# First W1 part of all eight experts loaded early and the chosen one copied; lower halves placed two blocks further

## The reference

```
# end of layer 0:  x = x + experts64(layernorm(x))        (router: layernorm(x) @ router_w.T)
# layer 1:
xn  = layernorm(x)
x   = x + gnn(xn) + mix(xn)        # gnn: agg @ W_conv, Wq, Wk, Wv, Wo, proj;  mix: w_qkv, w_proj
# last part of layer 1, E = 8, K = 2, FF = 2048
xe     = layernorm(x)
logits = xe @ Wg + bg
w, idx = top_k(logits, 2);  w = softmax(w)
h = silu(xe @ W1[e] + b1[e])       # W1: [8, 512, 2048]
y = h @ W2[e] + b2[e]              # W2: [8, 2048, 512]
out = x + sum over the two chosen e of w * y
```

## Time and profile before

| | us |
|---|---|
| median of 3 runs | 845.24 |
| lowest and highest of them | 845.07, 846.45 |
| the profiled execution | 843.48 |
| its span, first to last instruction | 841.7 |
| around the span | 1.78 |

### The profile page before, as it was taken

How to read it: one execution, slowest core, us unless ns; L and a number is a source line. 1 busy time by engine, 2 the same in 40 slices (tenths; PEclk the granted TensorE clock), 3 DMA queues, 4 the chain that set the end, 5 groups by cost and what they waited for, 6 DMA issues and landing times.

```text
span 841.7 us, 10823 instructions
## 1 busy us (share of the span) xinstructions
PE 800.7 (95%) x3995; PEld 640.9 (76%) x3995; DVE 539.5 (64%) x743; ACT 248.6 (30%) x468; POOL 148.2 (18%) x96
## 2 busy tenths in 40 slices
PE   4999999999999999999998999997699999999997
PEld 3988766847477777765767778897598888888886
DVE  5876998979989999999777426068541111511112
ACT  4252223316411013222045332142432321432310
POOL 2011001120100000002201350031343330433300
PEclk9999999999999998999999999999589999999999
DMA  7533779796878768742041120000242120322001
GB/s 245 213 50 47 227 214 337 266 276 158 240 228 276 246 220 282 242 139 100 1 159 58 48 97 1 1 2 1 100 151 96 55 98 2 100 100 100 0 0 61
DMA packets 64211, 110.21 MB, mean 131 GB/s; under 512 B 6815, under 2 KB 16412, under 8 KB 64172
## 3 DMA queue, kind: packets, MB, share of 16 engines
q1 hardware_dynamic: 54476, 96.71, 34.5%
q0 software_dynamic: 6912, 7.70, 5.4%
q10 hardware_dynamic: 2784, 5.27, 1.7%
HBM read 105.81 MB, written 1.28 MB: 127 GB/s over the span
## 4 chain that ended last, share of the span: by engine, by line
PE 89%; DVE 6%; issue 2%; ACT 1%; POOL 1%; DVEq 0%; POOLq 0%
PE bank L1310 55%; PE bank L1730 13%; PE bank L1396 6%; PE bank L1511 4%; PE bank L1528 3%; PE bank L1522 2%; PE bank L1505 2%; PE bank L1326 1%; DVE st L890 1%; PE bank L1437 1%; PE bank L1333 1%; DVE slot L987 1%; ACT slot L581 1%; DVE slot L885 0%; DVE slot L1116 0%
## 5 line engine op out<-in xcount | busy, mean ns | idle before, releaser
L1004 DVE SCALAR_TENSOR_TENSOR weights<-weights,att 128x2048 f32<-128x2048 f32 x116 | 268.9, 2392 | 2.7 <-DMA weights<-in_L_gnn_basis 2.1
L1291 DVE CAST hid_hi<-slot 128x626 fp32r<-128x626 f32 x32 | 15.6, 487 | 160.7 <-ACT slot L846 160.7
L1310 PE MATMUL bank<-half,ew_hi 128*128 128x314 f32 (+1 forms) x512 | 114.0, 312 | 2.2 <-POOL ew_lo L550 2.2
L1310 PE MATMUL bank<-AT,slot 125*128 125x312 f32 (+1 forms) x400 | 105.9, 426 | 0.8 <-ACT slot L711 0.8
L1310 PEld LDWEIGHTS bank<-AT,slot 125*128 125x128 f32 x400 | 75.5, 189 | 31.0 <-ACT slot L711 1.0
L550 POOL TENSOR_TENSOR ew_lo<-weights,ew_hi 128x1024 fp32r<-128x1024 f32 x28 | 69.4, 2500 | 134.4 <-ACT ew_hi L828 134.4
L1310 PEld LDWEIGHTS bank<-half,ew_hi 128*128 128x128 f32 x512 | 88.4, 193 | 5.6 <-issue 2.9
L581 ACT ACTIVATE slot<-bank 128x312 f32<-128x312 f32 (+6 forms) x88 | 43.8, 525 | 148.7 <-PE bank L1310 128.9
L1310 PE MATMUL bank<-weights,slot 128*125 128x512 f32 (+5 forms) x306 | 86.9, 447 | 0.3 <-ACT slot L581 0.3
L846 ACT ACTIVATE slot<-bank,eb_now 128x312 f32<-128x312 f32 x64 | 33.3, 522 | 157.2 <-PE bank L1310 157.2
L1310 PE MATMUL bank<-half,ew_lo 128*128 128x312 f32 (+1 forms) x256 | 79.5, 310 | 0.0
(11 more groups left out here) (297 smaller groups left out, 1116.4 us busy)
## 6 DMA issues: line engine op xcount, KB each, us to landing
weights<-in_L_gnn_basis SPq DMA_DIRECT2D x60, 1024.0 KB, 5.5
weights<-in_L_ffn_W SPq DMA_DIRECT2D x32, 512.0 KB, 4.5
weights<-in_L_mix_kqv_w SPq DMA_DIRECT2D x1, 3072.0 KB, 10.2
weights<-in_w_qkvT SPq DMA_DIRECT2D x3, 1024.0 KB, 5.4
slot<-slot POOLq DMA_DIRECT2D x10, 250.0 KB, 6.5
weights<-in_L_mix_mlp_w ACTq DMA_DIRECT2D x2, 1024.0 KB, 13.6
weights<-in_L_gnn_root ACTq DMA_DIRECT2D x2, 1024.0 KB, 8.7
slot<-in_row_mlp_b POOLq DMA_DIRECT2D x1, 1250.0 KB, 26.1
```

Of the source, the lines that this page charges most:

```text
L1004: ins = dve.scalar_tensor_tensor(wrel[layer][r], wmat(at), att[:, layer, r, b:b + 1], wrel[layer][r], ALU.mult, ALU.add)
L1310: ins = pe.matmul(out, a, b, start=i == 0, stop=i == len(pairs) - 1)
```

## The change

1. SP, once the product `xq` is complete, loads W1[e, :, 0:256] of all eight experts (512 KB each) to `candidates`, columns 8192 to 16383 of `weights`. When the list is there, it leaves out the W1 load of chunk 0 of the first expert.
2. DVE, behind the write of the expert numbers and ahead of the count, waits for these loads and for `lin_split` 4, reads the first expert's number into a register and copies its 1024 columns to raw chunk 0; the copy signals `ew_in0` in the place of the transfer.
3. So that `candidates` covers nothing live, the low part of block i lies at block (i + 2) % 4 of `ew_lo`, for the matrices and for the experts' chunks; `conv_hi` and `conv_lo` move to blocks 0 and 1.
4. Since `conv_hi` now lies where `o2` still reads, POOL's split of W_conv waits for `psum_full` at `filled("o2", 5)`, that is for the last tile of `o2`, where it waited for `o2_low` 4.

```
-        conv_hi, conv_lo = (ew_lo[:, b, :]... for b in (1, 2))
+        conv_hi, conv_lo = (ew_lo[:, b, :]... for b in (0, 1))
+        def low_block(i):
+            return ew_lo[:, (i + 2) % 4, :]
+        candidates = weights[:, 8192:8192 + 1024 * E1]
...
+            sp.wait_ge(S("psum_full"), filled("xq", 8))
+            for e in range(E1):
+                load(candidates[:, 1024 * e:1024 * e + 1024].rearrange("p (k f) -> p k f", k=KT),
+                     I["L1_ffn_W1"][e, :, 0:256].rearrange("(k p) f -> p k f", p=128), "cand_in")
             sp.wait_ge(S("elist"), 1)
             sp.wait_ge(S("lin_split"), 4)
...
-            def load_chunk(e, c):
+            def load_chunk(e, c, first=False):
                 w1c, w2c = raw1(c), raw2(c)
-                sp.dma_start(w1c, ...).then_inc(S(f"ew_in{c % 2}"), 16)
+                if not first:
+                    sp.dma_start(w1c, ...).then_inc(S(f"ew_in{c % 2}"), 16)
                 sp.dma_start(w2c, ...).then_inc(S(f"ew2_in{c % 2}"), 16)
...
             pool.wait_ge(S("Wconv_in"), 16)
-            pool.wait_ge(S("o2_low"), 4)
+            pool.wait_ge(S("psum_full"), filled("o2", 5))
             link(pool.tensor_copy(conv_hi, W_conv))
             pool.tensor_tensor(conv_lo, W_conv, conv_hi.bitcast(f32), ALU.subtract).then_inc(S("conv_split"), 1)
...
             dve.tensor_copy(el_i[0:1, 0:8], key1).then_inc(S("elist"), 1)
             dve.wait_ge(S("elist"), 1)
+            dve.wait_ge(S("cand_in"), 16 * E1)
+            dve.wait_ge(S("lin_split"), 4)
+            e = dve.value_load(el_i[0:1, 0:1], min_val=0, max_val=E1 - 1)
+            dve.tensor_copy(weights[:, 0:1024], candidates[:, bass.ds(1024 * e, 1024)]).then_inc(S("ew_in0"), 16)
             link(dve.tensor_scalar(srt, srt, 0.5, None, ALU.is_ge))
...
-                dve.tensor_tensor(ew_lo[:, 1, :], weights[:, 2048:4096], ew_hi[:, 1, :].bitcast(f32), ALU.subtract)...
+                dve.tensor_tensor(low_block(1), weights[:, 2048:4096], ew_hi[:, 1, :].bitcast(f32), ALU.subtract)...
```

More of the change, by code:

```diff
@@ L226, in gps_two_layers @@
         xb_hi, xb_lo = half[5], half[3]
-        conv_hi, conv_lo = (ew_lo[:, b, :].rearrange("p (k n) -> p k n", k=KT) for b in (1, 2))
+        conv_hi, conv_lo = (ew_lo[:, b, :].rearrange("p (k n) -> p k n", k=KT) for b in (0, 1))
         Z_AT = (5, 6)
@@ L232, in gps_two_layers, with lin_hi, lin_lo @@
         h1 = col(4)
-        def lin(t, name):
-            return t[:, LIN[name], :].rearrange("p (k n) -> p k n", k=KT)
+        def low_block(i):
+            return ew_lo[:, (i + 2) % 4, :]
+        candidates = weights[:, 8192:8192 + 1024 * E1]
+        def lin_hi(name):
+            return ew_hi[:, LIN[name], :].rearrange("p (k n) -> p k n", k=KT)
+        def lin_lo(name):
+            return low_block(LIN[name]).rearrange("p (k n) -> p k n", k=KT)
         def wait_split(eng, it, c, part=1):
@@ L249, in raw2, with w1_half, w2_half @@
             return wmat(2048 * (c % 2) + 1024, 2, H)
[L251 to L256, removed]
+        def w1_half(block, f):
+            return block[:, 0:1024].rearrange("p (k f) -> p k f", k=KT)[:, :, 128 * (f % 2):128 * (f % 2) + 128]
+        def w2_half(block, f):
+            return block[:, 1024 + H * (f % 2):1024 + H * (f % 2) + H]
         eb1 = sb("eb1", [128, E1 * F1 // 128])
@@ L412, in _ @@
             w2v = I["L1_ffn_W2"].rearrange("e (f p) n -> e p f n", p=128)
-            def load_chunk(e, c):
+            def load_chunk(e, c, first=False):
                 w1c, w2c = raw1(c), raw2(c)
-                sp.dma_start(w1c, w1v[bass.ds(e, 1), :, :, 256 * c:256 * c + 256].rearrange("o p k f -> (o p) k f")).then_inc(S(f"ew_in{c % 2}"), 16)
+                if not first:
+                    sp.dma_start(w1c, w1v[bass.ds(e, 1), :, :, 256 * c:256 * c + 256].rearrange("o p k f -> (o p) k f")).then_inc(S(f"ew_in{c % 2}"), 16)
                 sp.dma_start(w2c, w2v[bass.ds(e, 1), :, 2 * c:2 * c + 2, :].rearrange("o p f n -> (o p) f n")).then_inc(S(f"ew2_in{c % 2}"), 16)
@@ L423, in _ @@
                     wait_split(sp, 0, c - 2)
-                load_chunk(e, c)
+                load_chunk(e, c, first=c == 0)
             sp.wait_ge(S("elist"), 2)
@@ L511, in split_linear @@
             def split_linear(i, used):
-                hi, lo = (t[:, LIN[LIN_ORDER[i]], :] for t in (ew_hi, ew_lo))
+                hi, lo = ew_hi[:, LIN[LIN_ORDER[i]], :], low_block(LIN[LIN_ORDER[i]])
                 raw = weights[:, 2048 * (i % 2):2048 * (i % 2) + 2048]
@@ L549, in _ @@
                         pool.wait_ge(S("ew_high"), 16 * it + (2 * c + part + 1))
-                        pool.tensor_tensor(ew_lo[:, c % 4, at:at + 1024], weights[:, 2048 * (c % 2) + at:2048 * (c % 2) + at + 1024],
+                        pool.tensor_tensor(low_block(c)[:, at:at + 1024], weights[:, 2048 * (c % 2) + at:2048 * (c % 2) + at + 1024],
                                            ew_hi[:, c % 4, at:at + 1024].bitcast(f32), ALU.subtract).then_inc(S("ew_split"), 1)
@@ L1286, in _ @@
                 dve.wait_ge(S("ew_high"), 16 * it + 4)
-                dve.tensor_tensor(ew_lo[:, 1, :], weights[:, 2048:4096], ew_hi[:, 1, :].bitcast(f32), ALU.subtract).then_inc(S("ew_split1"), 1)
+                dve.tensor_tensor(low_block(1), weights[:, 2048:4096], ew_hi[:, 1, :].bitcast(f32), ALU.subtract).then_inc(S("ew_split1"), 1)
                 for f in range(16):
@@ L1360, in split_rows_out @@
             def split_rows_out(stage, name):
-                wh, wl = lin(ew_hi, name), lin(ew_lo, name)
+                wh, wl = lin_hi(name), lin_lo(name)
                 for j in range(TT):
@@ L1660, in _ @@
                 m, (a, w) = by_half(n)
-                split_cols(claim(pe, "xq", n), lin(ew_hi, "q"), lin(ew_lo, "q"), hid_hi, hid_lo, m, a).then_inc(S("psum_full"), 1)
+                split_cols(claim(pe, "xq", n), lin_hi("q"), lin_lo("q"), hid_hi, hid_lo, m, a).then_inc(S("psum_full"), 1)
             pe.wait_ge(S("xkv_out"), 1)
@@ L1673, in projected @@
                 pe.wait_ge(S("xo_low"), 4 * (n // 4) + 4)
-                split_cols(bk, lin(ew_hi, "proj"), lin(ew_lo, "proj"), hid_hi, hid_lo, m, a).then_inc(S("psum_full"), 1)
+                split_cols(bk, lin_hi("proj"), lin_lo("proj"), hid_hi, hid_lo, m, a).then_inc(S("psum_full"), 1)
             def sum_row(j):
@@ L1727, in output @@
                         hh, hl = (t[:, f % 4, P * j:P * j + P] for t in (hid_hi, hid_lo))
-                        products = ((hh, w2_half(ew_hi, f)), (hh, w2_half(ew_lo, f)), (hl, w2_half(ew_hi, f)))
+                        wh, wl = w2_half(ew_hi[:, f // 2 % 4, :], f), w2_half(low_block(f // 2), f)
+                        products = ((hh, wh), (hh, wl), (hl, wh))
                         for i, (a, b) in enumerate(products):
@@ L1740, in _ @@
                         pe.wait_ge(S("eh_out"), 32 * it + max(n - 2, 0) + 1)
-                        wh, wl = w1_half(ew_hi, f), w1_half(ew_lo, f)
+                        wh, wl = w1_half(ew_hi[:, f // 2 % 4, :], f), w1_half(low_block(f // 2), f)
                         group(B("eh", n % 3)[:, 0:w], [(wt[:, k, :], xt[:, k, a:a + w]) for k in range(KT)
```

## The result

Four runs of the changed kernel gave 852.37 us in the median (851.88 to 852.95), four of the kernel before 845.40 (845.07 to 846.45): a ratio of 1.0096, with a 95% interval of 1.0071 to 1.0122. The change makes the kernel slower. Measured once more beside later experiments, the ratio was 1.0048 (1.0030 to 1.0066). Where the runs of a kernel fall into groups the two can differ: e1's medians lie 3.4 us apart and its ratio is 1.0069, e6's lie 6.2 us apart and its ratio is 0.9958. The profiled execution took 852.95 us, its span 851.2.

The account below looks back on a forecast made before the run. The chain of work that ended last was taken as PE for 89% and DVE for 6%. Copy 1.5 + hold of DVE 3.1 + clock 1.0 = 5.6 us, against 845.24 giving 850.8 us; range 846.5 to 853.5.

Parts of the forecast that it names:

- a fall that covers a third of it: Router's stretch, 426.23 to 429.88 us: PE falls to 1.2 GHz for a third of it, 1.0 us.
- the rival with the fall over the whole stretch: Router's stretch: half clock throughout (2.9 us), or POOL keeps DVE out through both instructions (4.9 us); 852.7 us, chance 0.15.
- The hold of DVE: End of layer 0: POOL's late W_conv split blocks DVE's normalisations, delaying tile 3's transposes 3.1 us; ends 0 and 4.9.
- the second step: End of layer 0: tile 3's normalisation waits for POOL's subtraction until 428.85 us, ending near 429.2 instead of 426.09.
- The clock: Router's stretch: 3.6 us of idle PE may bring half clock; taken as 1.0 us, at most 2.9, at least 0.
- The copy: Start of the experts: DVE's register load (0.8) and copy (0.69) go wholly on the path, 1.5 us; ends 1.0 and 2.2.
- The loads at nothing: Behind the xq product: eight 512 KB loads on idle wires, some 38 us ahead of the expert list, cost nothing.
- the blocks at nothing: Low blocks in ew_lo: same engines, sizes and order, so the new places cost nothing.
- The early W1 off the path: Start of the experts: W1 had landed 1.7 us before ACT began, so loading it early gains the first product nothing.
- The ceiling I gave it, 1.06 us: Ahead of ACT's first high part: the most to be had if W1's landing did hold ACT, 1.06 us.
- The experts' start against the clock's rise, taken as 0: Experts' loop: it starts at another moment against the clock's rise; about 1 us either way, taken as 0.
- The rival in which L885 gets by: Router's stretch: DVE's normalisation is not held by POOL, only the copy's 1.5 us is left; 846.7 us, chance 0.11.

Follow-up runs that it names:

- e1: Kernel before with one line changed: POOL's W_conv split waits for the last o2 tile; no loads, copy or new blocks; 848.63 us, ratio 1.0069.
- e6: Layout of e2 without DVE's copy: ACT and POOL split the first expert's W1 chunk 0 straight from the candidates, ahead of the loop; 838.87 us, ratio 0.9958.
- e7: Changed kernel with 13 extra products on PE in the router's pause, ahead of the transposes of tile 3; 847.64 us, ratio 1.0045.
- e10: Kernel before with e1's late split and e7's 13 extra PE products in the pause, no loads or copy; 844.81 us, ratio 1.0004.
- e5: Changed kernel with POOL's late cast and subtraction of W_conv each cut into four pieces of 512 columns; 847.18 us, ratio 1.0033.
- e2: Changed kernel with the W_conv split back at its old time and blocks, the matrices' low parts in other blocks; 844.52 us, ratio 1.0009.
- e3: As e2, with DVE's register load and copy moved behind the write of the combination weights; 844.59 us against the kernel before, ratio 1.0001.
- e8: As e6, with extra PE products in the pauses from the expert transposes to the b2 products; 835.66 us, ratio 0.9910 against the kernel before.

## Why the prediction came out as it did

The direction was right, the mechanisms were those named, and the time, 852.37 us, lies inside the range of 846.5 to 853.5. The forecast of 850.8 was 1.6 us short, and the step at fault is one term of the sum: "I take 1.0, a fall that covers a third of it". It measured 3.4 us. No row stood behind the third; the rival with the fall over the whole stretch, 852.7 us at a chance of 0.15, is what happened.

- *The hold of DVE.* Forecast 3.1 us, measured 2.8 (e7 and e10, 31.87 and 31.85 against 29.07 us). The order was right: one TENSOR_SCALAR 0.3 us longer, in front of POOL's subtraction, then one behind the whole of it. The 0.3 us too much lie in the second step: by the profile POOL's subtraction began at 426.51 us, 0.2 us before the end of DVE's TENSOR_SCALAR, where I had put it behind. That one POOL instruction is what holds DVE, and that whoever waits goes first, e5 shows.
- *The clock.* Taken as 1.0 us with an upper end of 2.9. Measured: 3.1 us up to the COPY and 3.4 up to `aq`, over the end I had allowed. Two things were wrong. The fall covered all of the stretch in the two profiles of the changed kernel, not a third: that is 3.1 us. And I priced only the products up to the router's logits, while in these profiles the clock stayed low for 3 us behind the COPY too, which costs the other 0.3. e7 and e10, with PE busy in the same pause, have none of it. In e1 the first fall was the shorter one that I had in mind, 1.6 us up to the COPY, and a second fall near 451 us cost 1.7 more, which the sum had no term for.
- *The copy.* Forecast 1.5 us, measured 1.36, with a register load of 0.80 and a COPY of 0.69 as taken. That its whole price goes on the path e2 and e3 show, 14.08 and 12.69 us from logits to first product.
- *The loads at nothing* and *the blocks at nothing.* Right: in e3 the loads and the experts' low blocks cost nothing. The matrices' low blocks lie elsewhere in e3 than in the changed kernel; but from `aq` to the first product the two kernels with the copy take the same, 161.42 us with the one placing (changed) and 161.38 with the other (e2).
- *The early W1 off the path.* Right (e3: same 12.69 us). The ceiling I gave it, 1.06 us, holds for the load alone; with the splits behind it moved as well the whole was worth 2.4 us at the first product (e6), which I had not looked for.
- *The experts' start against the clock's rise, taken as 0.* In the changed kernel's profile it gave back 0.65 us (1.36 late at the first product, 0.7 at the end). The clock rose 4.59 us behind the first product, where it took 6.05.

Terms as measured in the traces: 2.8 + 3.4 + 1.36 - 0.65 = 6.9 us, the difference of the medians 7.0. Two things in this are luck. The forecast was only 1.6 us short because errors partly cancel: the clock is 2.4 us over its term, while the hold, the copy and the clock's rise together are 1.1 us under theirs. And the 7.0 are those of the first series; measured again the medians lay 4.3 us apart (849.93 and 845.65), which misses the forecast's 5.6 by as much on the other side. All four runs of the first series had a mean clock of 0.966, the five of the second 0.966 to 0.972: less of the half clock in most of them, and where it was missing is not shown. The rival of the longer fall was the nearest to what happened; its other half, POOL keeping DVE out through both instructions, did not. The rival in which L885 gets by falls with e1. The lower end of the range is put down as that rival's 846.5; its own sum gives 846.7, and nothing hangs on it.

## What to carry to other kernels

Before work is moved to a time when its engine is idle, look at what its neighbour does there: here a POOL subtraction of 4.6 us from SBUF to SBUF held the DVE TENSOR_SCALAR that came behind it until it ended, while an addition with one input from a bank was not held. So either such an instruction stays where DVE's work is not awaited, or it is cut into short pieces. A short hold on DVE can cost twice, when TensorE waits behind it and comes back at half clock. And an early load is worth only as much as the steps between it and its reader can follow: ask in whose queue the reader stands, and what it stands behind.

## What the runs showed that was not expected

- The price of a pause of TensorE is not fixed. In the changed kernel and in e1 PE idled for the same 3.21 us and came back 7.26 and 7.27 us behind the stretch's first transpose, and then took 6.78 us to the COPY in one and 5.24 in the other. e1 and e5 had a further fall near 451 us that neither before nor the changed kernel had. The falls that all kernels have near 169 and 193 us, at the same instructions, lasted 3.4 us in seven profiled executions, whose stretch begins at 420.4 to 421.7 us, and 6.8 in the five others, where it begins at 423.2 to 424.5 (first column of the table). The kernel before had runs from 841.1 to 847.5 us, mostly near 842.5 or near 846, and they go with the run's mean granted clock: in e1's series 841.1 to 842.2 us at 0.977, 841.7 to 843.1 at 0.974, 845.2 to 847.0 at 0.970 and 0.971, 846.2 to 846.9 at 0.968. So where two kernels differ by a few microseconds, their totals are to be read beside the mean clocks of the runs.
- So a stretch between two fixed instructions in which the clock does not fall came out the same to 0.02 us in five profiled executions (29.07 to 29.09), while totals of 5 to 12 runs could not settle 2.8 us (e10).
- Products whose result is never read made the kernel faster: 38 fp32 products of 128 columns in the pauses of e8 gave 4.6 us in the part behind `aq` (386.4 to 381.8).
